# A transformer block's attention loop on one Trainium2 core: key, query and weighing products moved to other steps

## The reference

```python
x = L0_attn_inputs                                        # (4, 256, 256) float32
x = x + 0.5 * ffn(layernorm(x), ...)                      # 8 experts, top 2
x = x + attn(layernorm(x), w_q, w_k, w_v, w_o, b_o)
x = x + 0.5 * ffn(layernorm(x), ...)

def attn(inputs, w_q, w_k, w_v, w_o, b_o):                # 16 heads of 16
    q, k, v = (inputs @ w.T for w in (w_q, w_k, w_v))     # reshaped (b, t, 16, 16)
    scores = einsum('bqhd,bkhd->bhqk', q, k)              # causal mask
    attn = softmax(scores / sqrt(t), axis=-1)
    ctx = einsum('bhqk,bkhd->bqhd', attn, v)
    return ctx.reshape(b, t, 256) @ w_o.T + b_o
```

## Time and profile before

| what | us |
|---|---|
| median of three runs | 420.56 |
| profiled execution, its own time | 420.87 |
| its span, first to last instruction | 419.1 |
| attention, from the first tail scores to the last weighing | 160.25 to 274.4 |
| busy over the span: PE, DVE, ACT, POOL | 380.4, 296.6, 256.6, 237.5 |

### The profile page before, as it was taken

One profiled execution on the slowest core, in us unless ns is written; L12 is line 12 of the kernel. 1 busy time (PEld: TensorE's weight loads), 2 busy tenths in 40 slices (PEclk: granted clock), 3 DMA queues, 4 the chain that ended last, 5 costly groups with the idle time before them and its releaser, 6 DMA issues.

```text
span 419.1 us, 9185 instructions
## 1 busy us (share of the span) xinstructions
PE 380.4 (91%) x2732; PEld 309.0 (74%) x2733; DVE 296.6 (71%) x620; ACT 256.6 (61%) x640; POOL 237.5 (57%) x307
## 2 busy tenths in 40 slices
PE   7769999999999989788888988797899999999996
PEld 3548888888888867566666766473788888888885
DVE  6878999555666796887777757967466765566566
ACT  2837865656555546799888878621455556555552
POOL 5255445565567359567878668201555545745860
PEclk9999999999999999899999989999999999999999
DMA  7949921112111620466867587819721111112126
GB/s 253 399 125 391 379 97 54 52 38 75 50 50 38 238 77 0 76 114 116 151 117 129 103 108 145 139 20 305 238 96 55 53 62 52 50 50 57 43 96 231
DMA packets 70929, 51.57 MB, mean 123 GB/s; under 512 B 53104, under 2 KB 64624, under 8 KB 70640
## 3 DMA queue, kind: packets, MB, share of 16 engines
q1 hardware_dynamic: 66064, 36.99, 34.3%
q0 software_dynamic: 4544, 12.07, 9.3%
q10 hardware_dynamic: 288, 2.10, 1.3%
HBM read 29.37 MB, written 9.19 MB: 92 GB/s over the span
## 4 chain that ended last, share of the span: by engine, by line
PE 57%; DMA 16%; DVE 15%; issue 4%; ACT 3%; POOL 2%; SPq 1%; DVEq 0%; ACTq 0%; POOLq 0%
PE bank L1408 27%; PE bank L1430 13%; DMA pT<-parts 5%; DMA w_raw<-in_win_t 4%; PE bank L1418 4%; PE bank L1580 3%; DMA pT<-parts_late 3%; PE bank L1547 3%; PE bank L1384 2%; DMA w_out<-y_scratch 2%; DVE x L1097 2%; DMA y_scratch<-arena,scatter_row 2%; DVE neg_max L1200 1%; PE bank L1617 1%; DVE parts L1214 1%
## 5 line engine op out<-in xcount | busy, mean ns | idle before, releaser
L546 POOL DMA_INDIRECT arena<-xn_scratch,gather_row x46 | 49.6, 1078 | 68.1 <-PE bank L1384 46.7
L552 POOL DMA_INDIRECT y_scratch<-arena,scatter_row x42 | 62.5, 1488 | 37.1 <-ACT arena L715 35.3
L1408 PE MATMUL bank<-w_hi,xT_hi 128*128 x184 | 61.7, 416 | 0.4 <-ACT xT_hi L674 0.4
L1058 DVE TENSOR_TENSOR wo_lo<-w_out,wo_hi 128x1024 fp32r<-128x1024 f32 x46 | 56.3, 1224 | 3.8 <-PE bank L1430 2.2
L1063 DVE TENSOR_TENSOR gT_lo<-bank,gT_hi 128x512 fp32r<-128x512 f32 x46 | 31.7, 690 | 38.1 <-ACT gT_hi L689 38.1
L1408 PE MATMUL bank<-w_hi,xT_lo 128*128 x184 | 57.5, 393 | 0.0
L1408 PE MATMUL bank<-w_lo,xT_hi 128*128 x184 | 57.3, 392 | 0.0
L682 ACT ACTIVATE arena<-bank 128x512 f32<-128x512 f32 x46 | 27.6, 599 | 45.6 <-PE bank L1408 45.6
L627 POOL TENSOR_TENSOR k_head<-k_hi,head_mask 128x256 fp32r<-128x256 f32 x64 | 38.7, 626 | 24.3 <-PE bank L1581 24.3
L704 ACT ACTIVATE wo_hi<-w_out 128x1024 fp32r x46 | 48.8, 1061 | 5.1 <-issue 3.0
L1580 PE MATMUL bank<-k_head,xT_hi 128*128 128x256 f32 (+1 forms) x128 | 40.2, 395 | 7.7 <-DVE parts L1214 5.9
(11 more groups left out here) (196 smaller groups left out, 915.5 us busy)
## 6 DMA issues: line engine op xcount, KB each, us to landing
w_raw<-in_win_t SPq DMA_DIRECT2D x8, 1024.0 KB, 10.9
w_out<-in_wout_t SPq DMA_DIRECT2D x16, 512.0 KB, 7.6
w_out<-y_scratch SPq DMA_DIRECT2D x8, 512.0 KB, 5.3
xn_scratch<-arena ACTq DMA_DIRECT2D x2, 1024.0 KB, 6.2
x<-in_x SPq DMA_DIRECT2D x4, 256.0 KB, 3.4
out<-x SPq DMA_DIRECT2D x4, 256.0 KB, 2.2
arena<-xn_scratch,gather_row POOLq DMA_INDIRECT x46, 3.4
y_scratch<-arena,scatter_row POOLq DMA_INDIRECT x46, 3.0
```

Of the source, the lines that this page charges most:

```text
L546: pool.indirect_dma_start(out=xb[j % 2][:, :], out_offset=None, in_=xn_dram, in_offset=bass.IndirectOffsetOnAxis(ap=gather_row[:, j:j + 1] ...
L552: pool.indirect_dma_start(out=y_dram, in_=y[j % 2][:, :], in_offset=None, out_offset=bass.IndirectOffsetOnAxis(ap=scatter_row[:, j:j + 1], ...
L1058: dve.tensor_tensor(wo_lo[:, :, :], w_out[:, bass.ds(e, 1), :, :].rearrange("p o c d -> p (o c) d"), wo_hi[u][:, :, :].bitcast(F32), ALU.s ...
L1408: last = pe.matmul(bank[2 * half + u][:, :], tok[u][:, k, :], wts[:, bass.ds(e, 1), k, half * H:(half + 1) * H], start=(part == 0 and k == ...
```

## The change

Keys and queries, made together in steps 0 and 3 in one bank, become two functions: keys in steps 0 and 3 in bank 7, queries in steps 1 and 4 in bank 4. The weighing of a pair comes four steps after its scores instead of three, and stands on PE between the tail and the head scores instead of behind both. The two sums over the context banks stand in step 5 on both sides of the head maxima and low half, with the reciprocal at the end of step 4. The turned context goes to bank 4; PE turns it at the end of step 6 and ACT copies it at the end of its step 6. The out-projection is cut in two halves in step 7, one ahead of the tail scores and one ahead of the head scores. The values of batch 0 use banks 3, 5 and 6. The last, draining call has one step more, with five warming products a step instead of six. POOL and SP keep their lists.

```diff
-VBANK = (3, 4, 5, 6, 5, 6, 5, 6)
+VBANK = (3, 5, 6, 5, 6, 5, 6, 5)
-CHUNK_STEP = (0, 3)
+KEY_STEP, QUERY_STEP = (0, 3), (1, 4)
-WARM_END = 6
+WARM_END = 5
...
-            return range(HPAIRS if new else SUM_STEP)
+            return range(HPAIRS if new else SLAG + 4)
...
             def step(b, old, new):
                 for s in steps_of(new):
-                    if old and s == OUT_STEP:
-                        act.wait_ge(ctxT_done, b)
-                        act.activation(ctxT[:, :, :], bank[7][:, :].rearrange("p (k t) -> p k t", k=DK), ACT.Copy,
-                                       scale=1.0 / P_SCALE).then_inc(ctxT_ready, 1)
                     if old if s < SLAG + 1 else new:
                         high(b, s)
                     if old if s < SLAG else new:
                         exps(b, s, True)
                     if not old and s == 0:
                         turn_out(1, (1,))
-                    if new and s in CHUNK_STEP:
-                        chunk(b, CHUNK_STEP.index(s))
+                    if new and s in KEY_STEP:
+                        key_chunk(b, KEY_STEP.index(s))
+                    if new and s in QUERY_STEP:
+                        query_chunk(b, QUERY_STEP.index(s))
                     if old if s < SLAG else new:
                         exps(b, s, False)
+                    if old and s == OUT_STEP:
+                        act.wait_ge(ctxT_done, b)
+                        act.activation(ctxT[:, :, :], bank[4][:, :].rearrange("p (k t) -> p k t", k=DK), ACT.Copy,
+                                       scale=1.0 / P_SCALE).then_inc(ctxT_ready, 1)
...
+            def invert(b):
+                sums = row_sum[:, b - 1, :, :]
+                dve.wait_ge(high_ready, b * HEADS)
+                reach(dve, ctx_ready, b - 1)
+                dve.reciprocal(inv_sum[:, :, :], sums).then_inc(inv_ready, 1)
+            def add_up(b, qt):
                 dve.wait_ge(pv_done, b * HEADS)
-                for qt in range(2):
-                    dve.tensor_reduce(ctxv[:, qt, :, :], bank[5 + qt][:, :].rearrange("p (h w d) -> p h d w", w=2, d=HD),
-                                      AX_X, ALU.add).then_inc(ctx_summed, 1)
...
             def step(b, old, new):
                 for s in steps_of(new):
-                    if old and s == SUM_STEP:
-                        add_up(b)
                     if old if s < SLAG else new:
                         maxima(b, s, True)
                     if old if s < SLAG + 1 else new:
                         low(b, s, True)
+                    if old and new and s == SUM_STEP:
+                        add_up(b, 0)
                     if old if s < SLAG else new:
                         maxima(b, s, False)
-                    if new and s in CHUNK_STEP:
-                        chunk(b, CHUNK_STEP.index(s))
+                    if new and s in KEY_STEP:
+                        key_chunk(b, KEY_STEP.index(s))
+                    if new and s in QUERY_STEP:
+                        query_chunk(b, QUERY_STEP.index(s))
                     if old if s < SLAG + 1 else new:
                         low(b, s, False)
+                    if old and new and s == SUM_STEP - 1:
+                        invert(b)
+                    if old and new and s == SUM_STEP:
+                        add_up(b, 1)
...
+            def key_chunk(b, c):
+                reach(pe, k_lo_ready, b * DK + c)
+                for k in range(DK):
+                    last = pe.matmul(bank[7][:, 0:SEQ], wk[:, k, c * P:(c + 1) * P], xnT[:, k, b * SEQ:(b + 1) * SEQ],
+                                     start=(k == 0), stop=(k == DK - 1))
+                last.then_inc(k_done, 1)
+            def query_chunk(b, c):
+                reach(pe, q_ready, b * DK + c)
+                if c == 0:
                     reach(pe, attn_added, b)
-                for w, to in ((wq, 0), (wk, SEQ)):
-                    for k in range(DK):
-                        last = pe.matmul(bank[7][:, to:to + SEQ], w[:, k, c * P:(c + 1) * P], xnT[:, k, bass.ds(b * SEQ, SEQ)],
-                                         start=(k == 0), stop=(k == DK - 1))
-                last.then_inc(qk_done, 1)
+                for k in range(DK):
+                    last = pe.matmul(bank[4][:, 0:SEQ], wq[:, k, c * P:(c + 1) * P], xnT[:, k, b * SEQ:(b + 1) * SEQ],
+                                     start=(k == 0), stop=(k == DK - 1))
+                last.then_inc(q_done, 1)
...
-                g = b * HPAIRS + (s - SLAG - 3)
-                ago = s < SLAG + 3
-                turned = pT[(s - 1) % 2]
+                g = b * HPAIRS + (s - SLAG - 4)
+                ago = s < SLAG + 4
+                turned = pT[g % 2]
                 pe.wait_ge(pT_ready[g % 2], g // 2 * 16 + 16)
...
-            def project_out(b):
+            def project_out(b, qt):
                 pe.wait_ge(ctxT_ready, b)
-                for qt in range(2):
-                    for c in range(DK):
-                        last = pe.matmul(bank[7][:, qt * D:(qt + 1) * D], ctxT[:, c, qt * P:(qt + 1) * P], wo[:, c, :],
-                                         start=(c == 0), stop=(c == DK - 1))
-                last.then_inc(o_done, 1)
+                for c in range(DK):
+                    last = pe.matmul(bank[4][:, qt * D:(qt + 1) * D], ctxT[:, c, qt * P:(qt + 1) * P], wo[:, c, :],
+                                     start=(c == 0), stop=(c == DK - 1))
+                if qt:
+                    last.then_inc(o_done, 1)
             def step(b, old, new):
                 for s in steps_of(new):
-                    if old and s == OUT_STEP + 1:
-                        project_out(b)
+                    if old and new and s == OUT_STEP + 1:
+                        project_out(b, 0)
                     if old if s < SLAG else new:
                         scores(b, s, True)
...
-                    if old and s == OUT_STEP:
-                        turn_context(b, new)
-                    if new and s in CHUNK_STEP:
-                        chunk(b, CHUNK_STEP.index(s))
-                    if not old and s == SLAG + 1:
...
-                    if old if s < SLAG else new:
-                        scores(b, s, False)
-                    if old if s < SLAG + 3 else new:
-                        if s == SLAG + 3:
+                    if old if s < SLAG + 4 else new:
+                        if s == SLAG + 4:
                             if old:
                                 pe.wait_ge(ctx_summed, b * 2)
...
                         weigh(b, s)
+                    if new and s in KEY_STEP:
+                        key_chunk(b, KEY_STEP.index(s))
+                    if new and s in QUERY_STEP:
+                        query_chunk(b, QUERY_STEP.index(s))
+                    if old and new and s == OUT_STEP + 1:
+                        project_out(b, 1)
+                    if not old and s == SLAG + 1:
+                        pe.wait_ge(v_rest_ready, 1)
+                    if old if s < SLAG else new:
+                        scores(b, s, False)
+                    if old and new and s == OUT_STEP:
+                        turn_context(b, new)
```

More of the change, by code:

```diff
@@ L323, in build @@
         v_ready = sem("v_ready")
-        qk_done = sem("qk_done")
-        qk_hi_ready = sem("qk_hi_ready")
+        q_done = sem("q_done")
+        k_done = sem("k_done")
+        q_hi_ready = sem("q_hi_ready")
         k_hi_ready = sem("k_hi_ready")
         k_lo_ready = sem("k_lo_ready")
-        qk_ready = sem("qk_ready")
+        q_ready = sem("q_ready")
         k_head_ready = sem("k_head_ready")
@@ L1182, in _, with key_chunk, query_chunk @@
             scale(1, TPAIRS - 1)
-            def chunk(b, c):
-                dve.wait_ge(qk_hi_ready, b * DK + (c + 1))
-                dve.tensor_tensor(k_lo[:, c, :], bank[7][:, SEQ:2 * SEQ], k_hi[:, c, :].bitcast(F32), ALU.subtract)\
+            def key_chunk(b, c):
+                dve.wait_ge(k_hi_ready, b * DK + (c + 1))
+                dve.tensor_tensor(k_lo[:, c, :], bank[7][:, 0:SEQ], k_hi[:, c, :].bitcast(F32), ALU.subtract)\
                     .then_inc(k_lo_ready, 1)
-                dve.scalar_tensor_tensor(q_lo[c][:, :, :], bank[7][:, 0:SEQ].rearrange("p (q t) -> p q t", q=2),
-                                         1.0 / SEQ ** 0.5, q_hi[c][:, :, :].bitcast(F32),
-                                         ALU.mult, ALU.subtract).then_inc(qk_ready, 1)
+            def query_chunk(b, c):
+                scaled = bank[4][:, 0:SEQ].rearrange("p (q t) -> p q t", q=2)
+                dve.wait_ge(q_hi_ready, b * DK + (c + 1))
+                dve.scalar_tensor_tensor(q_lo[c][:, :, :], scaled, 1.0 / SEQ ** 0.5, q_hi[c][:, :, :].bitcast(F32),
+                                         ALU.mult, ALU.subtract).then_inc(q_ready, 1)
             def maxima(b, s, tail):
@@ L1215, in low @@
```

(16 more changed lines are left out.)

24 lines of the change are left out of this document (11 added, 13 removed).

## The result

The changed kernel took 429.26 us (median of 4, 425.92 to 431.4) against 420.14: ratio 1.021, interval 1.014 to 1.028. The change is slower in both: +9.1 and +5.7. The forecast had 425.0, +4.4, and its range ended at 428.8, +8.2: the first median lies beyond it, the second within.

The account below looks back on a forecast made before the run. ACT was taken to bound a batch; a walk of its waits gave 26.85 us against 25.21, +4.9 for three. With -0.3 for batch 0, 420.87 became 425.5, by median 425.2, said as 425.0; own range 422.8 to 427.5, outer 417 to 428.8.

Parts of the forecast that it names:

- 0.95: Ahead of step 2's tail exponentials: its tail scores wait for q_lo, a new ACT wait of 0.95 us.
- 0.42: Step 3, keys: head exponentials start at 10.70 against ACT free at 9.08 + 1.20, a wait of 0.42 us.
- 0.23: Ahead of step 5's tail exponentials: tail maxima follow q_lo, low head and reciprocal, a wait of 0.23 us.
- 0.6: Step 5: the first context sum stands ahead of the head maxima, making head exponentials 0.6 us late.
- 0.2: Step 6: the weighing waits for the second sum and holds the head scores, head exponentials 0.2 us late.
- 2.0: Ahead of step 7's tail exponentials: the out-projection's first half waits for the context's copy, a new wait of 2.0 us.
- 0.62: Step 7: the out-projection's second half delays the head maxima, so head exponentials wait 0.62 us.
- Slack 0.7: Tightest pT transfer, step 0's pair: lands at 10.2, weighed in step 4 at 10.9, 0.7 us to spare.
- the clock, put at nothing: PE's clock falls got no term in the sum; a clock gain or loss was left to rivals.
- batch 0, put at -0.3: Batch 0: no context to project, a small transfer wait goes, values run while DVE is behind: -0.3 us.
- rival 3: PE's longer pauses around the out-projection lower the clock: 2.1 more in two batches, 429; with two other rivals 0.15.
- Rival 1: Steps 6 and 7: out-projection input early or exponentials late enough to hide it; batch 24.2, total 415.5 us; chance 0.17.

Follow-up runs that it names:

- e16: The changed kernel itself, unchanged, timed again on another chip: 427.88 us, ratio to before 1.014.
- e12: The kernel before with three warming products ahead of the weighings of steps 2 and 5: 421.55 us, ratio to before 1.001.
- e13: e8 with 3 and 12 warming products ahead of the tail scores of steps 5 and 6 of batch 0: 419.15 us, ratio to before 0.994.
- e2: The changed kernel with both out-projection halves behind the head scores of step 7: 433.07 us, ratio to before 1.026.
- e7: The changed kernel with out-projection behind step 7's head scores, division behind its masks, query products, copy and q_lo earlier in steps 1 and 4: 419.01 us, ratio 0.995.
- e8: e7 with both sums over the context banks behind the low head of step 5: 418.81 us, ratio to before 0.994.

## Why the prediction was right in sign and wrong in size

- *ACT bounds a batch, and each new wait on it is time:* right. The step lengths of a clean batch (2.71, 3.66, 2.54, 3.04, 2.94, 3.05, 5.17, 3.14) each stand within 0.2 of the walk's (2.80, 3.75, 2.53, 3.22, 3.03, 3.12, 5.25, 3.2). Of its waits 0.95 measured 0.67, 0.42 measured 0.32, 0.23 none, 0.6 measured 0.50, 0.2 some 0.17, 2.0 measured 2.01, 0.62 measured 0.59. The batch came out 26.25, not 26.85 (the terms as written add up to 26.83).
- *Transfers:* "Slack 0.7" was near enough; waits of PE of 0.2 to 0.7 came in some steps of batches 1 and 3, where "no wait of PE on pT" was forecast, and make 27.83 and 26.62 of e16's batches. So the waits alone are 80.7 - 76.25 (the sum of e12's batches) = 4.5 of three batches, against the forecast's 4.9.
- *The steps that failed are two terms of the sum: the clock, put at nothing, and batch 0, put at -0.3.* The profiled execution lies 4.2 over the 425.5 of the sum: 2.7 are the clock's, 2.0 are batch 0's, and the waits give 0.4 back.
- *The clock.* The sum had as many falls after as before, the rest was left to rival 3 with part of 0.15, and so the range ended under the first median. Instead two falls in steps 6 and 7 made three batches 84.8, against 80.7 without them in e16: 4.1. The one fall of before made them 77.7, against 76.25 in e12: 1.4. The reason given against it (batch 1 of before waited and kept its clock) set unlike waits side by side: 1.06 in batch 1, and in batch 3, PE's timeline of before:

```profile
243.90 0.21 PE L1596 MATMUL bank<-v,pT 128*128 128x32 bf16 x1 [1.57 <-DMA pT<-parts]
```

  The new pauses that the walk itself had found in steps 6 and 7 were the argument for the term. The waits ahead of both falls were for other engines, 0.7 to 1.0 each. The Trainium skill (TensorE: Matmul & The Clock Gate, section A second HAM failure mode: psum-queue depth-cycling) has a second case beside the waits for transfers that the prediction drew on: a kernel in which "the PE micro-idles between MM groups frequently enough that HAM oscillates". The trace of the first profile agrees in two batches of three; e16's, with the same waits, in none.
- *Batch 0.* It was -0.5 in e16 and +1.7 in the first profile. The prediction saw a wait for a transfer go and DVE behind, and didn't ask how long DVE's splits of the values take while POOL writes masks. DVE's and POOL's timelines, the first profile and then e16's:

```profile
171.23 1.17 DVE L1306 TENSOR_TENSOR v<-v_rest,v 128x256 bf16<-128x256 f32 x2
171.45 1.41 POOL L628 TENSOR_TENSOR k_head<-k_hi,head_mask 128x256 fp32r<-128x256 f32 x2 [2.22 <-PE bank L1609]
```

```profile
172.62 0.75 DVE L1306 TENSOR_TENSOR v<-v_rest,v 128x256 bf16<-128x256 f32 x2
174.06 1.18 POOL L628 TENSOR_TENSOR k_head<-k_hi,head_mask 128x256 fp32r<-128x256 f32 x2 [3.43 <-PE bank L1609]
```

  In all 18 profiles a pair of these splits takes 1.17 us or more where POOL's masks run beside most of it, and 0.75 where none does; two pairs of the first profile's batch 0 are such places, at 171 and at 176. In e16 a fall of the clock at 171 made the head scores late, and with them the masks; DVE was through by then. The batch is 23.2 to 24.3 in the three profiles with a fall at 168 to 172 (before, e13, e16) and 24.7 to 25.9 in the fifteen others, with a fall at 178 to 181 or with none. So a fall there is no loss, and the single profiles of before and after stood on different sides of this. Without the early fall it is 24.74 (e12, before's batch 0) against 24.9 to 25.4 (the change's), so the term is rather +0.1 to +0.7 than -0.3.
- *What is luck.* By its ratio the second timing puts the change at 420.56 x 1.014 = 426.4, 1.4 over the forecast and inside its range. The one execution of 426.12 lies 0.6 from the sum's 425.5 by chance: its attention part is only 2.5 longer than that of before's profile, and the rest, put at 0, is 2.8 longer.
- *Rival 1* put the way to a faster kernel in one gate, the copy. There were two; the sentence on POOL's masks and division, "in time by over 0.5", failed, as e2 shows. With both lifted the batch is 24.9, near the 24.2 of the rival, and with the query copy 24.0.
- What stays open: why filling the pauses gave back clock but hardly time, how often the clock falls in steps 6 and 7, and so how the 5.7 to 9.1 us between the medians divide. The waits' 4.5 are shown. The clock's 2.7 and batch 0's 2.0 are read from single profiles, and its 1.1 to 3.8 over all executions are inferred.

## What to carry to other kernels

Before moving work ahead of another engine's input, list everything that gates the next critical instruction: two gates that open together hide each other, and lifting one looks worthless or worse. A named releaser is not yet the cause: the addition that waited in front of the maxima was not what held them. Where the walk of a change finds new pauses of PE, its range has to hold the clock's falls too, at the high end. The fastest form found here (e7; e8 and e13 can't be told from it) keeps the weighing's new place and the split banks, with the out-projection behind the scores, the division behind the masks and the query copy ahead of the exponentials: ratio 0.995 (0.993 to 0.997).

## What was not expected of the hardware

One program on one core ran with no fall of PE's clock in its steps 6 and 7 in one profiled execution and with two in another: 426.12 us and 429.68, though the waits in front were the same (0.71 and 1.04 in the one, 0.71 and 0.99 in the other). The fall of batch 1 came in the microsecond of which PE was busy 0.37, after pauses of 0.73 and 0.71, and lasted 7 us; before's fall of batch 3, after a pause of 1.57, lasted 4. And a lower clock isn't always time lost: of this kernel's batch 0 the profile with a fall at 171 took 23.16 us, those with a fall at 178 to 181 took 24.9 to 25.4, in part because two pairs of DVE's splits took 0.75 us in the one, without POOL's masks beside them, and 1.17 in the others.
